# Layer 0's aggregate of the next batch as three fp32r products, with its copies at the end of the round

## The reference

```
layer 0: agg = eps * h + adj @ h;  out = silu(rmsnorm(agg @ W1 + b1)) @ W2 + b2     (W1: 256 x 1024)
layer 1: attention by sigmoid(s1 + s2 + b) * adj, rows normalised, times h @ W + b
layer 2: 8-head attention (softmax, masked by adj, edge bias adj * w_e), then @ W_o
layer 3: (D^-1/2 adj D^-1/2) @ (h @ W) + bias
```

## Time and profile before

| | us |
|---|---|
| median of 3 runs | 3615.05 |
| lowest, highest | 3612.17, 3615.54 |
| the profiled execution | 3618.28 |
| its span, first to last instruction | 3616.5 |

### The profile page before, as it was taken

The page is one execution under the profiler, slowest core; times in us unless marked ns, Lnnn a source line. Parts: engine busy times, 40 slices in busy tenths (PEclk is TensorE's granted clock), DMA queues, the critical chain, the costliest instruction groups (busy, mean ns, idle before and its releaser), DMA issues.

```text
span 3616.5 us, 70003 instructions
## 1 busy us (share of the span) xinstructions
PE 3473.8 (96%) x19886; PEld 2554.9 (71%) x20108; DVE 2666.2 (74%) x6666; ACT 2285.3 (63%) x5062; POOL 958.2 (26%) x2379
## 2 busy tenths in 40 slices
PE   6999999999999999999999999999999999999997
PEld 5767677767777776777677777767776677777674
DVE  6777777777777777777777777777777777777774
ACT  4666566666676666666666666666666666666664
POOL 2223331222322233322232222333222332122320
PEclk8999999999999999999999999999999999999999
DMA  3233223232232332232322323322323222233212
GB/s 101 51 90 88 75 64 86 60 93 72 71 84 58 88 91 72 64 92 53 93 76 71 81 64 82 93 70 65 92 53 93 78 71 78 69 77 93 70 54 64
DMA packets 166942, 275.09 MB, mean 76 GB/s; under 512 B 23909, under 2 KB 59877, under 8 KB 166761
## 3 DMA queue, kind: packets, MB, share of 16 engines
q1 hardware_dynamic: 166760, 273.45, 28.5%
HBM read 122.37 MB, written 16.78 MB: 38 GB/s over the span
## 4 chain that ended last, share of the span: by engine, by line
PE 70%; DVE 10%; issue 9%; ACT 6%; DMA 2%; SPq 2%; DVEq 0%; POOL 0%; ACTq 0%; POOLq 0%
PE turn L1331 8%; PE value L1346 6%; PE score L1372 6%; PE front L1226 6%; PE front L1164 6%; PE score L1322 6%; PE front L1134 5%; PE front L1135 5%; PE front L1136 5%; PE score L1319 3%; ACT prob L634 2%; DMA qk_stack<-qk 2%; DVE prob L982 2%; PE front L1191 2%; PE score L1362 2%
## 5 line engine op out<-in xcount | busy, mean ns | idle before, releaser
L634 ACT ACTIVATE prob<-prob,small 128x512 f32<-128x512 f32 x1024 | 736.4, 719 | 374.4 <-DVE small L982 370.6
L982 DVE CUSTOM_DVE_ANT_0 prob<-score,adj_sb,drv 128x512 f32<-128x512 f32 x1024 | 757.8, 745 | 81.8 <-PE score L1322 70.1
L1331 PE MATMUL turn<-ident,prob 128*128 128x128 f32 x4096 | 625.5, 275 | 37.5 <-DVE pT L991 24.6
L1322 PE MATMUL score<-qk_stack 128*128 128x512 f32 x1024 | 592.8, 583 | 10.5 <-DMA qk_stack<-qk 10.5
L1331 PEld LDWEIGHTS turn<-ident,prob 128*128 128x128 f32 x4096 | 481.6, 141 | 158.2 <-issue 41.8
L643 ACT ACTIVATE pT<-turn 128x512 f32<-128x512 f32 x768 | 449.5, 585 | 97.9 <-PE turn L1331 69.7
L742 DVE TENSOR_TENSOR s_lo<-front,s_hi 128x512 fp32r<-128x512 f32 x316 | 216.6, 686 | 168.5 <-ACT s_hi L533 168.5
L1319 PE MATMUL score<-unlinked,neg_mask 128*128 128x512 bf16 x802 | 306.4, 382 | 20.1 <-DVE small L982 18.4
L1134 PE MATMUL front<-w_hi,s_hi 128*128 128x256 f32 x1024 | 300.4, 293 | 0.0
L442 POOL TENSOR_TENSOR small<-small 128x1 f32<-128x1 f32 x128 | 25.9, 202 | 996.6 <-ACT aside L574 996.6
L1135 PE MATMUL front<-w_lo,s_hi 128*128 128x256 f32 x1024 | 288.7, 282 | 0.0
(11 more groups left out here) (203 smaller groups left out, 7972.2 us busy)
## 6 DMA issues: line engine op xcount, KB each, us to landing
qk_stack<-qk SPq DMA_DIRECT2D x1024, 128.0 KB, 2.4
adjT_f<-in_adjT SPq DMA_DIRECT2D x32, 1024.0 KB, 5.3
adj_sb<-in_adj SPq DMA_DIRECT2D x32, 1024.0 KB, 7.4
prob<-in_adjT SPq DMA_DIRECT2D x32, 1024.0 KB, 5.4
x_new<-in_x SPq DMA_DIRECT2D x32, 512.0 KB, 4.8
out<-x_out SPq DMA_DIRECT2D x32, 512.0 KB, 3.0
pT<-in_W SPq DMA_DIRECT2D x2, 1024.0 KB, 11.2
rmsw_b<-in_rmsw SPq DMA_DIRECT2D x1, 512.0 KB
```

Of the source, the lines that this page charges most:

```text
L634: act.activation(prob[:, i % 8, :], prob[:, i % 8, :], ACT.Exp, bias=nmax[:, h, n:n + 1], scale=-1.0, accum_out=prsum[:, h, n:n + 1]).then ...
L982: dve.tensor_tensor_reduce(out=prob[:, i % 8, :], in0=SB_[i % 2][:, :], in1=adj_sb[:, n, :], scale=neg_w[:, h:h + 1], scalar=3e38, op0=ALU ...
L1322: pe.matmul(SB_[i % 2][:, :], qk_stack[:, h % 4, 0, tile(n)], qk_stack[:, h % 4, 1, :], start=False, stop=True).then_inc(sc_ps, 1)
L1331: last = pe.transpose(TB[k % 2][:, tile(n)], prob[:, (4 * h + n) % 8, tile(j)], ident[:, :])
```

## The change

It makes four new tiles, all over `pT`: `af_hi` and `af_lo` (high and low part of `adjT_f`, 2048 columns each), `h_hi` and `h_lo` (of `h0`, 1024 columns each). ScalarE makes both high parts in one instruction each, VectorE makes `af_lo` in one, GpSimd makes `h_lo` in one. TensorE makes the aggregate from three sets of eight fp32r products, h_hi x af_hi and h_lo x af_hi in the place of `aggregate(nx, 0)`, h_hi x af_lo in the place of `aggregate(nx, 1)`. Both halves are complete only after the last set, so `T_hi` and `T_lo` of both halves are made at the end. VectorE's `diagonal(nx)` moves ahead of `attended1(tf, 1)`. The batch 0 aggregate ahead of the rounds stays in fp32.

```diff
+        af_hi = sb("af_hi", [P, NT, N], F32R, over="pT")
+        af_lo = sb("af_lo", [P, NT, N], F32R, over="pT", skip=4 * 2048)
+        h_lo = sb("h_lo", [P, NT, D], F32R, over="pT", skip=4 * 4096)
+        h_hi = sb("h_hi", [P, NT, D], F32R, over="pT", skip=4 * 7168)
 # GpSimd
+            def rows_low(nx):
+                pool.wait_ge(h_hi_ready, at(nx, 1, 0))
+                pool.tensor_tensor(h_lo[:, :, :], h0, h_hi[:, :, :].bitcast(F32), ALU.subtract).then_inc(h_lo_ready, 1)
...
                 if t is not None:
                     add_b3(t)
+                if nx is not None:
+                    rows_low(nx)
 # ScalarE
+            def rows_high(nx):
+                act.wait_ge(f_norm["ready"], at(nx, 8, 4))
+                hi(h_hi[:, :, :], h0).then_inc(h_hi_ready, 1)
+
+            def adjacency_high(nx):
+                act.wait_ge(diag_eps, at(nx, 1, 1))
+                act.wait_ge(att_added, at(nx, 3, 0))
+                hi(af_hi[:, :, :], adjT_f[:, :, :]).then_inc(af_hi_ready, 1)
...
                     norm0(nx)
+                    rows_high(nx)
                 if b:
                     gathered(t, 0)
+                if nx is not None:
+                    adjacency_high(nx)
+                if b:
                     gathered(t, 1)
                 if f:
                     layernorm(tf, 0, b_norm, norm_tiles(50), x2, hf)
+                    turned(tf)
                 if nx is not None:
                     aggregated(nx, 0)
-                if f:
-                    turned(tf)
-                if nx is not None:
                     aggregated(nx, 1)
 # VectorE
+            def adjacency_low(nx):
+                dve.wait_ge(af_hi_ready, at(nx, 1, 0))
+                lo(af_lo[:, :, :], adjT_f[:, :, :], af_hi[:, :, :]).then_inc(af_lo_ready, 1)
...
                     attended1(tf, 0)
+                if nx is not None:
+                    diagonal(nx)
+                if f:
                     attended1(tf, 1)
                     factors1(tf)
-                if nx is not None:
-                    diagonal(nx)
-                if f:
                     update1(tf)
                 if b:
                     gathered(t, 0)
                     gathered(t, 1)
                 if nx is not None:
-                    aggregated(nx, 0)
+                    adjacency_low(nx)
                 if f:
                     turned(tf)
                 if b:
                     update3(t)
                 if nx is not None:
+                    aggregated(nx, 0)
                     aggregated(nx, 1)
                     restore_diagonal(nx)
 # TensorE
+            def aggregate_high(nx):
+                pe.wait_ge(h_hi_ready, at(nx, 1, 0))
+                pe.wait_ge(af_hi_ready, at(nx, 1, 0))
+                pe.wait_ge(msg_ready, at(nx, 4, 0))
+                for d in range(DT):
+                    for m in range(NT):
+                        pe.matmul(FB[d][:, :], h_hi[:, m, tile(d)], af_hi[:, m, :], start=(m == 0), stop=False)
+                pe.wait_ge(h_lo_ready, at(nx, 1, 0))
+                for d in range(DT):
+                    for m in range(NT):
+                        pe.matmul(FB[d][:, :], h_lo[:, m, tile(d)], af_hi[:, m, :], start=False, stop=False)
+
+            def aggregate_low(nx):
+                pe.wait_ge(af_lo_ready, at(nx, 1, 0))
+                for d in range(DT):
+                    for m in range(NT):
+                        last = pe.matmul(FB[d][:, :], h_hi[:, m, tile(d)], af_lo[:, m, :], start=False, stop=(m == NT - 1))
+                    last.then_inc(agg_ps, 1)
...
                 if nx is not None:
-                    aggregate(nx, 0)
+                    aggregate_high(nx)
...
                 if nx is not None:
-                    aggregate(nx, 1)
+                    aggregate_low(nx)
```

More of the change, by code:

```diff
@@ L170, in gnn_kernel @@
         table_in = sem("table_in")
+        h_hi_ready, h_lo_ready, af_hi_ready, af_lo_ready = (
+            sem(n) for n in ("h_hi_ready", "h_lo_ready", "af_hi_ready", "af_lo_ready"))
         unlinked_ready, deg_ready = sem("unlinked_ready"), sem("deg_ready")
@@ L1094, in phases @@
                     attended1(tf, 0)
-                    attended1(tf, 1)
-                    factors1(tf)
                 if nx is not None:
@@ L1099, in phases @@
                 if f:
+                    attended1(tf, 1)
+                    factors1(tf)
                     update1(tf)
```

## The result

The changed kernel takes **3629.32 us** (median of 6 runs, 3627.98 to 3630.38); the kernel before, beside it, 3615.36 (6 runs). The ratio is 1.0039, with a 95% interval of 1.0027 to 1.0051: slower by 14 us. The forecast was 3619, inside a range of 3581 to 3635.

The account below looks back on a forecast made before the run. TensorE, busy 96%, was taken as the bound. A gain of 1.27 us a round, eaten by stalls of 0.3 and 1.07, left +0.12, times 30 is 3.6 us: 3619 us forecast, range 3581 to 3635.

Parts of the forecast that it names:

- rival A: Same two VectorE/GpSimd conflicts, port held longer: 0.58 us a round, 3633 us; chance 0.14.
- Products: TensorE's aggregate: 24 fp32r products at 0.234 us replace 8 fp32 ones at 0.86, saving 1.27 us a round.
- `h_hi`, `af_hi`: ScalarE's high-part copies take 1.04 and 1.90 us, hidden before TensorE needs them.
- `h_lo` on GpSimd: Takes 2.35 us, delays VectorE's first update by 1.22 us, so aggregate_high starts 0.3 us late.
- `af_lo`: On VectorE, 2.29 us; holds GpSimd's last norm instruction, stalling TensorE's last two turns by 1.07 us.
- End of the stretch: On TensorE, aggregate_low ends at 1649.79 against 1649.67, so a round grows 0.12 us.
- moving `diagonal` gains nothing: VectorE's diagonal ahead of attended1(1): no gain in a full round, as update1 waits for TensorE; no cost either.
- 0, give or take 1.5: First round: h_lo delays the aggregate about 1 us, earlier diagonal and cheaper second part give about that back.
- The step that failed: Start of next round: VectorE's 2.10 us wait and TensorE's 0.32 us idle hang on the last T_lo, moving with it.
- B: GpSimd's last norm instruction slips ahead of af_lo, or af_lo comes later; only 0.3 remains: 3586 us; chance 0.13.
- C: h_lo does not hold VectorE's update, af_lo still holds GpSimd's norm; stall of 0.16 us: 3582 us; chance 0.07.
- D: Neither VectorE/GpSimd conflict occurs: -38 us, 3577 us; chance 0.05.

Follow-up runs that it names:

- e7: Changed kernel with 64 semaphore increments added at the start of VectorE's program; 3610.89 us.
- e10: Kernel before with 64 semaphore increments added at the start of VectorE's program; 3611.01 us.
- e9: Changed kernel with 64 semaphore increments added at the start of ScalarE's program; 3627.95 us (one run).
- e8: Kernel before with two semaphore increments added at the start of VectorE's program; 3626.05 us.
- e3: Changed kernel without GpSimd's h_lo, TensorE multiplying h_hi a second time in its place; 3593.15 us.
- e4: Changed kernel in which VectorE's af_lo also waits for GpSimd's last norm factor of layer 2; 3602.48 us.
- e11: Changed kernel with h_lo on VectorE ahead of af_lo, and 64 increments at the start of VectorE's program; 3597.38 us.
- e14: Changed kernel with 64 VectorE increments and h_lo on VectorE, ahead of the two low parts of layer 3's aggregate; 3568.52 us.
- e5: Changed kernel with h_lo made by VectorE, ahead of af_lo, and not by GpSimd; 3614.57 us.
- e13: Changed kernel with af_lo also waiting for GpSimd's last norm factor, and 64 increments at the start of VectorE's program; 3587.38 us.

## Why the prediction was half right

The range held the time, and each step in the edited stretch came out. The likeliest class, no change to be told (0.38, against 0.35 for slower), did not: the kernel is 0.39% slower. That the range held is in part luck. The loss comes from a mechanism that neither the sum nor a rival had (0.07 was kept for something unseen), and its 11 us happened to fit below the 3635 that rival A had set.

- **Products**: 0.234 us each was forecast. The first eight start at 1642.93, the second eight at 1644.86: 1.93 / 8 = 0.24.
- **`h_hi`, `af_hi`**: 1.04 and 1.90 forecast, 1.06 and 1.91 measured, both hidden.
- **`h_lo` on GpSimd**: 2.35 forecast, 2.42 measured; the first update ends 1.31 late and not 1.22. `aggregate_high` starts at 1639.40 in the clock of before; 1639.5 was forecast.
- **`af_lo`**: start 1641.84 (1641.86 forecast); the fourth L431 ends at 1644.17 (1644.20); the last two turns start at 1644.86 (1644.97). The stall in the turns is there, 0.89 us by the profile against 1.07.
- **End of the stretch**: `aggregate_low` starts at 1647.87 and its eight products of 0.234 end at 1649.74: +0.07 against the forecast +0.12. At nearly like code (e7 and e10) a round differs by 0.01 us and the first by nothing, so "moving `diagonal` gains nothing" and the first round's "0, give or take 1.5" agree with the sum, though neither was tried alone.
- **The step that failed**: "The next wait, VectorE's 2.10 us between `restore_diagonal` and the first `qk` low part and then the stacked DMA on which TensorE idles 0.32 us, hangs on that `T_lo` and moves with it." The `T_lo` moved by 0.04 us and the stacked product by 0.93. The instructions added to VectorE's program shift every block boundary of its code, and one of them moved onto the score transfers. The prediction held that no DMA changes its place on SyncE's or any other queue; the engines' own code is a DMA traffic that it didn't count. It also took from the row that VectorE's 2.10 us are a wait for `qk`, which had come 1.6 us before. The late product is worth 0.43 us a round at the mask-and-minimum (8.50 - 8.07); the rest of the round gained 0.07, which leaves the 0.36 by which a round grew, 11 us in 30 rounds. The first round added 1.0; it also moves by as much in runs that don't touch it (82.0 in e9, 82.6 in e8), so no cause is given for it.

**The rivals.** A, whose 3633 lies nearer the measured time than the forecast's 3619, isn't what happened: the long L972 and L431 were as in the forecast's case, not longer. L972 ended 0.28 us behind `h_lo`, less than its own 0.48, and `af_lo` did not wait out the instruction ahead of the long L431: it began at 1645.37, 0.30 before L429 ended. B, C and D fell with those two rows. e3 and e4 show that the prices behind C and B were right: without the first conflict 36 us less (33 + 4 by the forecast), without the second 27 less (29 + 4). In e4 VectorE also stopped at a block boundary of its code, so that the mask-and-minimum came at 8.79 us and not 8.50: 0.29 x 30 = 9 us, more than the 6 that are missing.

The Trainium skill ("SBUF — State Buffer", Who interferes with whom) has VectorE with two SBUF inputs and GpSimd's reads exclude each other, while one SBUF input does not contend. The trace agrees on both for the long overlaps: 1.79 and 1.95 us beside `h_lo` and `af_lo`, 0.19 us under `a_lo`. It doesn't bear out the exclusion for a whole instruction: in 30 of 31 rounds `af_lo` begins 0.3 us before the recorded end of the fourth L429 (1645.12 and 0.55), which has its two inputs in SBUF, and takes 2.28 us all the same. Recorded spans of GpSimd are rough, so this is no more than a sign.

## What to carry to other kernels

Ahead of comparing two versions of a looped kernel to within half a per cent, compare where the instruction packets fall in the round, and run each version with some idle instructions ahead of its loop, less what these take themselves (0.1 us each): two of them were worth 10 us here, of the 14 that the edit appeared to cost. Give an operation with two SBUF inputs to VectorE or GpSimd only where the other has nothing due, or put it behind a wait: a wait of 0.6 us on purpose earned 0.9 a round. And when an operand is moved to another engine, its place in that engine's order matters as much as the engine: 29 us between e11 and e14.

## What the hardware did that was not expected

- With a packet of 8 KB of instructions at 6.0 to 6.4 us in the round, the transfer for which TensorE waits lands 3.1 us after its issue; with the packet at 9.3 or at 26 to 27, 2.4 us after it.
- With the boundary two instructions earlier still (e4 and e5), VectorE itself stops early in the round: its degree sum comes 5.9 us after the restore in e5, against 4.9 in the changed kernel and, with the 64 increments, in e11; in e4 6.2, against 5.2 in e13.
- The same boundary cost the kernel before 0.36 us a round between the product and the mask-and-minimum (1.07 us against 0.71 in e10), in which VectorE itself stood still with its wait over. Why that long wasn't tried.
- Three of the five packets of a round are VectorE's, by their moving: with the 64 increments of e7 they start at 26.9, 61.5 and 97.9 us in place of 6.1, 42 and 82, and the increments of TensorE and ScalarE moved none. Whose those at 0.5 and 3 are, no run shows.
